# Causal attention in a decoder: the keys' turn one group later, a prologue in another order, and value products three groups back

## The chip, the cores and the metric

The kernel runs on one NeuronCore of a Trainium2 chip. The metric is the device time of one launch in microseconds, the median of several runs. Beside it stands one profiled execution, from which all rows below are read. Engines are named as in the profile: PE is TensorE (matmuls, and transposes as matmuls with the identity), PEld its weight loads, DVE is VectorE, ACT is ScalarE, POOL is GpSimd, SP is the engine that issues the DMAs.

## The reference, cut to what matters

The kernel computes two decoder layers on 8 batches of 256 tokens of width 512: linear attention, a convolution mixer, a feed-forward block, then causal attention, a cross attention and a mixture of small experts, each followed by a residual and a normalisation. The change touches the causal attention alone:

```python
qkv = jnp.einsum('bsd,de->bse', x, Wqkv)
q, k, v = jnp.split(qkv, 3, axis=-1)
q = _layernorm_scale_only(q, q_ln_scale)          # over all 512 columns
k = _layernorm_scale_only(k, k_ln_scale)
...                                               # 16 heads of 32
scores = jnp.einsum('bshd,bthd->bhst', q / jnp.sqrt(jnp.float32(HEAD_DIM)), k)
scores = jnp.where(causal, NEG_INF, scores)
attn = jax.nn.softmax(scores, axis=-1)
ctx = jnp.einsum('bhst,bthd->bshd', attn, v)
out = jnp.einsum('bsd,de->bse', ctx.reshape(B, S, D_MODEL), out_W)
```

## The kernel before

The stage is the function `l1_attention`. Each engine has its own instruction list, written out by hand, and the engines meet only through counting semaphores (`wait_ge`); nothing reorders them. A batch (b = 0 to 7) has 256 tokens, two halves of 128 (t = 0, 1), and is worked in four groups (g = 0 to 3) of four heads. `steps()` runs over all 32 groups, n = 4b + g.

While the groups of batch b are worked, batch b + 1 is made ready. A unit (`project`) is a projection of one half by a 512-column part of the weights, 12 matmuls (three passes over four blocks: high by high, high by low, low by high part). Units 0 to 3 are queries and keys of half 0, then queries and keys of half 1; units 4 and 5 are the values. They write two banks, `p_ps[0]` and `p_ps[1]`, in turn. Queries and keys are normalised: VectorE takes mean and variance and writes the centred rows (`centre`, L1494 to L1502), POOL makes the reciprocal deviation (`rstds`), ACT scales the keys with it (`keys`, L1417), TensorE turns queries and keys (`turn_q` L1661, `turn_k` L1668), and ACT and VectorE copy the turned tiles out (`turned_q` L1421, `turned_k` L1507). The queries' deviation is applied later, as the scale of the exponentials.

A group n goes through: `scores` (L1683) into the four banks of `s_ps`; `masked_scores` (L1513) on VectorE, which copies them to SBUF; `maxima` of each half; `exps` on ACT, four heads for each half (L1433); `reciprocals` on VectorE; `normalise` on POOL (L1390, half 1 of group n - 1 and half 0 of group n at step n); `turn_p` (L1697), three transposes of four heads each, of group n - 2; `copy_pt` on ACT (two) and VectorE (one); `values` (L1712) of group n - 2 at the end of step n; `round_out` on ACT (L1447) and `lo_out` on VectorE (L1542), which split the output in a high and a low part. Once a batch the output projection (`output`), the residual and the normalisation follow.

PSUM is full: `p_ps` two banks, `s_ps` four, `tr_ps` and `v_out_ps` one each. Turned tiles (x, q, k, p) borrow the banks of `s_ps` between two groups' scores (`in_spare`), so the next group's scores wait until every borrowed bank is copied out:

```python
if n:
    pe.wait_ge(masked, n)
for h in range(GH):
    if h in freed:
        pe.wait_ge(*freed.pop(h))
```

Weights come in 8 pieces through a ring of three buffers: two each for Wq, Wk, Wv and Wout. ACT rounds a piece (`round_hi`, L107) and VectorE takes what is left (`take_lo`, L112); the first three are loaded ahead, during the stage before.

Of the kernel before, what the change touches and what calls it, by code (L numbers as in the profile page):

```python
# [14 lines left out]
P = 128  # L15
B, S, D = 8, 256, 512
T = S // P
# [1233 lines left out]
def l1_attention(core, ahead, after, x, y, q_scale, k_scale):  # L1251
    nc = core.nc
    with ExitStack() as ctx:
# [39 lines left out]
        q_bank, k_bank = spare[2], spare[3]  # L1293
# [20 lines left out]
        def unit_count(b, t):  # L1314

            return t + 1 if b == 0 else 4 + t if b == 1 else 4 * b + t - 1

        def residual_count(b):

            return 4 * b + 10 if b < B - 2 else 31 + b - (B - 2)  # L1320

# [6 lines left out]
        with nc.Block() as block:  # L1328
# [30 lines left out]
            def _(pool):  # L1359
# [12 lines left out]
                def rstds(b, t):  # L1372
                    n, u = T * b + t, b % 2
                    pool.wait_ge(mv_done, 2 * n + 2)
# [32 lines left out]
            def _(act):  # L1407
# [5 lines left out]
                def keys(b, t):  # L1413
                    n = T * b + t
                    act.wait_ge(rstd_done, n + 1)
                    act.wait_ge(p_free[1], unit_count(b, t))
                    act.activation(kn[t][:], kn[t][:], ACT.Copy, scale=rstd[:, t, 1:2]).then_inc(kn_done, 1)  # L1417

                def turned_q(b, t):
                    act.wait_ge(q_turned, T * b + t + 1)  # L1420
                    act.activation(qT[b % 2][:, :, t, :], q_bank, ACT.Copy).then_inc(q_copied, 1)  # L1421
# [26 lines left out]

                for r in range(2):
                    round_x(0, r)  # L1450
                split.round_hi(act, 0, len(split.pieces))
                for t in range(T):
                    keys(0, t)
                    turned_q(0, t)
                for t in range(T):
                    values(0, t)
                for r in range(2):
                    round_x(1, r)
                for b, u, g, n in steps():
                    if n >= 3:  # L1460
                        round_out(n - 3)
                    exps(b, u, n, 0)
# [12 lines left out]
                    if g == 2 and b + 1 < B:  # L1475
                        values(b + 1, 1)
                last = NG * B - 1
# [7 lines left out]
            def _(dve):  # L1485
# [5 lines left out]
                def centre(b, t, i):  # L1491
                    n, out, row = T * b + t, (qn, kn)[i][t], (qs_row, ks_row)[i]
                    dve.wait_ge(p_mm, 6 * b + 2 * t + i + 1)
                    dve.bn_stats(st[:, t, i, :], p_ps[i][:]).then_inc(st_done, 1)  # L1494
                    if b:
                        dve.wait_ge(ve_done, n - 1)
                    dve.wait_ge(st_done, 2 * n + i + 1)
                    dve.bn_aggr(mv[:, t, i, :], st[:, t, i, :]).then_inc(mv_done, 1)
                    dve.wait_ge(mv_done, 2 * n + i + 1)
                    if b:  # L1500
                        dve.wait_ge((q_turned, k_turned)[i], n - 1)
                    dve.scalar_tensor_tensor(out[:], p_ps[i][:], mv[:, t, i, 0:1], row[:], ALU.subtract, ALU.mult)\  # L1502
                       .then_inc(p_free[i], 1)

                def turned_k(b, t):
                    dve.wait_ge(k_turned, T * b + t + 1)
                    dve.tensor_copy(kT[b % 2][:, :, t, :], k_bank).then_inc(k_copied, 1)  # L1507
# [44 lines left out]

                for r in range(2):
                    lo_x(0, r)
                split.take_lo(dve, 0, 4)
                dve.wait_ge(rows_loaded, 32)
                for i in range(2):
                    centre(0, 0, i)
                split.take_lo(dve, 4, len(split.pieces))
                for i in range(2):  # L1560
                    centre(0, 1, i)
# [3 lines left out]
                for r in range(2):  # L1565
                    lo_x(1, r)
                for b, u, g, n in steps():
# [16 lines left out]
                    if g in (1, 2) and b + 1 < B:  # L1584
                        turned_k(b + 1, g - 1)
# [6 lines left out]
                    if g == 1 and b >= 2:  # L1592
                        norm.apply(dve, b - 2)
                last = NG * B - 1
# [14 lines left out]
            def _(pe):  # L1609
# [25 lines left out]
                def project(b, unit):  # L1635
                    u = b % 2
                    i, t = (unit % 2, unit // 2) if unit < 4 else (2, unit - 4)
# [19 lines left out]
                def turn_q(b, t, n=0):  # L1657
                    in_spare(2, n, q_copied, T * b + t + 1)
                    pe.wait_ge(p_free[0], unit_count(b, t))
                    for g in range(NG):  # L1660
                        last = pe.transpose(q_bank[:, g, :], qn[t][:, g * P:(g + 1) * P], core.ident[:])  # L1661
                    last.then_inc(q_turned, 1)

                def turn_k(b, t, n=0):
                    in_spare(3, n, k_copied, T * b + t + 1)
                    pe.wait_ge(kn_done, T * b + t + 1)
                    for g in range(NG):
                        last = pe.transpose(k_bank[:, g, :], kn[t][:, g * P:(g + 1) * P], core.ident[:])  # L1668
# [50 lines left out]
                for unit in range(6):  # L1719
                    pe.wait_ge(split.lo_done, (2, 4, 4, 4, 6, 6)[unit])  # L1720
                    project(0, unit)
                for t in range(T):
                    turn_q(0, t)
                    turn_k(0, t)
                for r in range(2):
                    turn_x(1, r)
# [744 lines left out]
```

## Time and profile before

| | us |
|---|---|
| median of three runs | 2142.49 (2141.91 to 2142.78) |
| profiled execution, its own time | 2137.15 |
| its span, first to last instruction | 2135.3 |
| TensorE busy | 1864.2 (87%) |
| VectorE busy | 1249.0 (58%) |
| ScalarE busy | 920.2 (43%) |
| GpSimd busy | 288.9 (14%) |
| mean granted clock of TensorE | 0.946 of full speed |

The shares are means over six stages. The causal stage runs from 1258.9 us to about 1684 us of the span. In a timeline row the first number is the start, the second the duration, xN the number of instructions merged, and the bracket at the end gives the idle time of the engine just before and what ended it. A table by stretch gives for each engine its busy time and count, then the granted clock (1.00 is 2.4 GHz, 0.50 is 1.2 GHz), the share of the DMA engines and GB/s.

### The profile page before, as it was taken

The page shows a single profiled execution, that of the slowest core. Times are in us where ns is not written, and L with a number is a line of the kernel's source. Part 1 is how long each engine was busy: PE and PEld are TensorE (multiplying, and loading weights), DVE is VectorE, ACT ScalarE, POOL GpSimd, SP SyncE. Part 2 cuts the span into 40 slices and gives each one's busy share as a digit, 9 for nine tenths or more (in the row PEclk, how much of TensorE's full clock was granted, in tenths as well). Part 3 has the DMA queues.
Part 4 walks back from the last instruction along what each step waited for, and adds up shares of the span by engine and source line. Part 5 has one row for each costly group of instructions (what it writes and reads, how often), then busy time and mean ns, then how long its engine had stood idle before and what let it go on. Part 6 is the DMA issues. An engine that isn't in the chain of part 4 may idle for free. (4 is left out here: it accounts for less than half of the span.)

```text
span 2135.3 us, 33023 instructions
## 1 busy us (share of the span) xinstructions
PE 1864.2 (87%) x12272; PEld 1514.4 (71%) x12272; DVE 1249.0 (58%) x2330; ACT 920.2 (43%) x2376; POOL 288.9 (14%) x347
## 2 busy tenths in 40 slices
PE   6979999999966899999999967888887488889966
PEld 5869999998954788888888855666665355555543
DVE  3445444444425665654565335677776378878847
ACT  2234333333323433333332224555556388888821
POOL 0000000000001111211111001223333221111001
PEclk9989999999988899999999988899998799999988
DMA  3122000000122221111110121000001377465234
GB/s 101 51 89 70 21 21 21 21 21 21 35 60 79 84 65 40 45 35 31 40 40 16 40 80 40 11 31 31 31 20 41 112 194 173 125 159 138 80 112 138
DMA packets 86253, 136.62 MB, mean 64 GB/s; under 512 B 9480, under 2 KB 25480, under 8 KB 86096
## 3 DMA queue, kind: packets, MB, share of 16 engines
q1 hardware_dynamic: 86096, 134.52, 21.8%
q8 instruction: 99, 1.62, 0.3%
q14 instruction: 58, 0.48, 0.1%
HBM read 79.88 MB, written 21.05 MB: 47 GB/s over the span
## 5 line engine op out<-in xcount | busy, mean ns | idle before, releaser
L1941 ACT ACTIVATE e_p<-e_s_ps,e_nb 128x512 f32<-128x512 f32 x256 | 174.8, 696 | 50.7 <-DVE e_nb L1989 49.2
L1164 PE MATMUL yp<-ccy,toep 128*128 128x288 f32 x640 | 178.7, 429 | 19.7 <-POOL ccy L892 13.6
L1433 ACT ACTIVATE p<-p,nb,rq 128x128 f32<-128x128 f32 (+1 forms) x256 | 136.8, 540 | 121.0 <-DVE nb L1524 121.0
L1989 DVE TENSOR_REDUCE e_nb<-e_s_ps 128x2 f32<-128x1024 f32 x128 | 155.7, 1217 | 50.9 <-PE e_s_ps L2066 50.9
L2076 PE MATMUL e_t_ps<-ident,e_p 128*128 128x128 f32 x1024 | 145.8, 281 | 23.8 <-DVE e_pT L1996 12.8
L1164 PEld LDWEIGHTS yp<-ccy,toep 128*128 128x128 f32 x640 | 124.0, 202 | 54.5 <-POOL ccy L892 14.8
L2076 PEld LDWEIGHTS e_t_ps<-ident,e_p 128*128 128x128 f32 x1024 | 117.9, 144 | 60.3 <-issue 50.3
L80 PE MATMUL q_ps<-a_xt_hi,wq_hi 128*128 128x256 f32 x512 | 151.9, 297 | 4.1 <-DVE wo_lo L112 4.1
L1062 DVE SCALAR_TENSOR_TENSOR hm<-gu_ps,us_col,sg 128x256 f32<-128x256 f32 x88 | 42.3, 481 | 182.0 <-ACT sg L971 182.0
L82 PE MATMUL q_ps<-a_xt_hi,wq_lo 128*128 128x256 f32 x512 | 146.6, 286 | 0.0
L81 PE MATMUL q_ps<-a_xt_lo,wq_hi 128*128 128x256 f32 x512 | 146.5, 286 | 0.0
L514 ACT ACTIVATE ex<-ex 128x512 f32<-128x512 f32 x64 | 40.4, 632 | 214.1 <-DVE ex L567 214.1
L1390 POOL TENSOR_TENSOR p<-p,rs 128x512 f32<-128x512 f32 x64 | 94.1, 1470 | 246.8 <-DVE rs L1531 246.8
L231 POOL TENSOR_TENSOR n_rstd<-n_mv,eps 128x2 f32<-128x2 f32 x32 | 6.2, 195 | 894.3 <-DVE n_mv L225 894.3
L971 ACT ACTIVATE sg<-gu_ps,gs_col 128x256 f32<-128x256 f32 x88 | 41.5, 472 | 188.1 <-PE gu_ps L82 188.1
L545 DVE TENSOR_TENSOR tl<-t_ps,th 128x512 fp32r<-128x512 f32 x64 | 44.2, 691 | 132.6 <-ACT th L506 132.6
L80 PE MATMUL o_ps<-wo_hi,th 128*128 128x512 f32 x256 | 106.7, 417 | 1.9 <-DVE tl L545 1.9
L80 PE MATMUL gu_ps<-m_xt_hi,wg_hi 128*128 128x256 f32 x352 | 100.1, 285 | 8.2 <-DVE m_xt_lo L1054 8.2
L2066 PE MATMUL e_s_ps<-ks,qs 128*128 128x512 f32 x256 | 95.3, 455 | 13.1 <-DMA ks<-e_cl 11.9
L80 PEld LDWEIGHTS q_ps<-a_xt_hi,wq_hi 128*128 128x128 f32 x512 | 100.1, 195 | 4.5 <-issue 4.5
L567 DVE TENSOR_SCALAR ex<-q_ps,bq_col 128x256 f32<-128x256 f32 x128 | 55.8, 477 | 80.3 <-PE q_ps L82 80.3
L81 PE MATMUL o_ps<-wo_lo,th 128*128 128x512 f32 x256 | 101.2, 395 | 0.0
(277 smaller groups left out, 5167.5 us busy)
## 6 DMA issues: line engine op xcount, KB each, us to landing
x_after<-n_r SPq DMA_DIRECT2D x24, 512.0 KB, 3.0
toep<-padded_kernels SPq DMA_DIRECT2D x32, 256.0 KB, 3.4
qs<-e_xh SPq DMA_DIRECT2D x64, 128.0 KB, 2.6
qs<-e_xl SPq DMA_DIRECT2D x64, 128.0 KB, 2.6
ks<-e_ch SPq DMA_DIRECT2D x64, 128.0 KB, 2.6
ks<-e_cl SPq DMA_DIRECT2D x64, 128.0 KB, 2.6
x<-x_after SPq DMA_DIRECT2D x12, 512.0 KB, 4.6
x<-in_x SPq DMA_DIRECT2D x8, 512.0 KB, 4.0
```

The lines of the kernel that those rows point to most:

```text
L80: pe.matmul(out, whi, xhi, start=start, stop=False)
L81: pe.matmul(out, whi, xlo, start=False, stop=False)
L82: return pe.matmul(out, wlo, xhi, start=False, stop=stop)
L545: dve.tensor_tensor(tl[:], t_ps[:], th[:], ALU.subtract).then_inc(tl_done, 1)
L567: dve.tensor_scalar(ex[p % 2][:, h, :], q_ps[p % 2][:, h, :], bq_col[:, head:head + 1], 0.0, ALU.add, ALU.min).then_inc(mq_done, 1)
L1164: last = pe.matmul(yp[:, lo % 2, 0:NCOL], toep[h % 2][:, (lo - li) * P:(lo - li + 1) * P], ccy[h % 2][:, li, 0:NCOL], start=(li == 0), sto ...
L1390: pool.tensor_tensor(tile, tile, r, ALU.mult).then_inc(pn_done, 1)
L1433: act.activation(p[n % 3][:, h, part[t]], p[n % 3][:, h, part[t]], ACT.Exp, bias=nb[i][:, t, h:h + 1], scale=rq[u][:, t:t + 1], accum_out= ...
L1941: act.activation(pr[i][:, a, :], s_ps[i][:, a, :], ACT.Exp, bias=nb[i][:, a:a + 1], accum_out=sums[t][:, j, q:q + 1]).then_inc(e_done, 1)
L1989: dve.tensor_reduce(nb[i][:], s_ps[i][:], AX.X, ALU.max, negate=True).then_inc(nb_done, 1)
L2066: last = pe.matmul(s_ps[i][:, a, :], qs[u][:, h // HT, h % HT, q * P:(q + 1) * P], ks[u][:, h // HT, h % HT, :], start=True, stop=True)
L2076: last = pe.transpose(t_ps[a][:, k, :], pr[m % 2][:, a, k * P:(k + 1) * P], core.ident[:])
```

## The change

It has four parts, which all engines' lists follow.

1. `turn_k` and `turned_k` of batch b + 1 move from groups 1 and 2 to groups 2 and 3.
2. `values` moves from the end of a step, where it took group n - 2, to behind the scores, where it takes group n - 3. On ACT `round_out(n - 3)` moves behind `exps` of half 0.
3. The prologue (batch 0) projects queries of both halves, then keys, then values, with queries of half t in bank t and keys of half t in bank t; the turns use the bank of `s_ps` numbered t. Pieces 0 and 1 of the weights are split ahead of x, and x of batch 1 is turned between the queries' turn and the values.
4. The last two weight pieces (Wout) are split at the end of groups 1 and 2 of batch 0, on ACT and VectorE, no more in the prologue.

```diff
@@ -1290,7 +1290,8 @@
         part = (slice(0, P), slice(P, P + S))
         spare = [s_ps[:, h, :].rearrange("p (a n) -> p a n", a=NG) for h in range(GH)]
         p_bank_of = [tr_ps[:], spare[0], spare[1]]
-        q_bank, k_bank = spare[2], spare[3]
+        q_bank = lambda b, t: spare[2 if b else t]
+        k_bank = lambda b, t: spare[3 if b else t]
 
         s = lambda n: core.sem("d_" + n)
         rows_loaded, set_up, mask_zeroed, xr_loaded = s("rows_loaded"), s("set_up"), s("mask_zeroed"), s("xr_loaded")
@@ -1311,13 +1312,21 @@
                 for g in range(NG):
                     yield b, b % 2, g, NG * b + g
 
-        def unit_count(b, t):
-
-            return t + 1 if b == 0 else 4 + t if b == 1 else 4 * b + t - 1
+        def unit_count(b, i, t):
+
+            return i + 1 if b == 0 else 4 + t if b == 1 else 4 * b + t - 1
 
         def residual_count(b):
 
             return 4 * b + 10 if b < B - 2 else 31 + b - (B - 2)
+
+        def unit_bank(b, i, t):
+
+            return t if b == 0 or i == 2 else i
+
+        def unit_place(b, i, t):
+
+            return 6 * b + (T * i + t if b == 0 or i == 2 else 2 * t + i)
 
         def x_half(g):
             return {0: 0, 3: 1}[g]
@@ -1371,7 +1380,7 @@
 
                 def rstds(b, t):
                     n, u = T * b + t, b % 2
-                    pool.wait_ge(mv_done, 2 * n + 2)
+                    pool.wait_ge(mv_done, 2 * n + 2 if b else 3 + t)
                     if n >= T:
                         pool.wait_ge(kn_done, n - 1)
                     pool.tensor_tensor(rstd[:, t, :], mv[:, t, :, 1], eps1[:], ALU.add).then_inc(ve_done, 1)
@@ -1413,12 +1422,12 @@
                 def keys(b, t):
                     n = T * b + t
                     act.wait_ge(rstd_done, n + 1)
-                    act.wait_ge(p_free[1], unit_count(b, t))
+                    act.wait_ge(p_free[unit_bank(b, 1, t)], unit_count(b, 1, t))
                     act.activation(kn[t][:], kn[t][:], ACT.Copy, scale=rstd[:, t, 1:2]).then_inc(kn_done, 1)
 
                 def turned_q(b, t):
                     act.wait_ge(q_turned, T * b + t + 1)
-                    act.activation(qT[b % 2][:, :, t, :], q_bank, ACT.Copy).then_inc(q_copied, 1)
+                    act.activation(qT[b % 2][:, :, t, :], q_bank(b, t), ACT.Copy).then_inc(q_copied, 1)
 
                 def values(b, t):
                     act.wait_ge(p_mm, 6 * b + 4 + t + 1)
@@ -1446,20 +1455,22 @@
                         act.wait_ge(o_mm, T * (b - 1))
                     act.activation(oh[b % 2][:, g, :], v_ps[:], ACT.Copy).then_inc(oh_done, 1)
 
+                split.round_hi(act, 0, 2)
                 for r in range(2):
                     round_x(0, r)
-                split.round_hi(act, 0, len(split.pieces))
+                split.round_hi(act, 2, 6)
+                for t in range(T):
+                    turned_q(0, t)
+                for r in range(2):
+                    round_x(1, r)
                 for t in range(T):
                     keys(0, t)
-                    turned_q(0, t)
                 for t in range(T):
                     values(0, t)
-                for r in range(2):
-                    round_x(1, r)
                 for b, u, g, n in steps():
+                    exps(b, u, n, 0)
                     if n >= 3:
                         round_out(n - 3)
-                    exps(b, u, n, 0)
                     if g in (1, 2) and b + 1 < B:
                         keys(b + 1, g - 1)
                     if n >= 2:
@@ -1474,6 +1485,8 @@
                     exps(b, u, n, 1)
                     if g == 2 and b + 1 < B:
                         values(b + 1, 1)
+                    if n in (1, 2):
+                        split.round_hi(act, 5 + n, 6 + n)
                 last = NG * B - 1
                 round_out(last - 2)
                 for n in (last - 1, last):
@@ -1490,21 +1503,23 @@
 
                 def centre(b, t, i):
                     n, out, row = T * b + t, (qn, kn)[i][t], (qs_row, ks_row)[i]
-                    dve.wait_ge(p_mm, 6 * b + 2 * t + i + 1)
-                    dve.bn_stats(st[:, t, i, :], p_ps[i][:]).then_inc(st_done, 1)
+                    place, bank = unit_place(b, i, t), unit_bank(b, i, t)
+                    centred = 4 * b + place - 6 * b
+                    dve.wait_ge(p_mm, place + 1)
+                    dve.bn_stats(st[:, t, i, :], p_ps[bank][:]).then_inc(st_done, 1)
                     if b:
                         dve.wait_ge(ve_done, n - 1)
-                    dve.wait_ge(st_done, 2 * n + i + 1)
+                    dve.wait_ge(st_done, centred + 1)
                     dve.bn_aggr(mv[:, t, i, :], st[:, t, i, :]).then_inc(mv_done, 1)
-                    dve.wait_ge(mv_done, 2 * n + i + 1)
+                    dve.wait_ge(mv_done, centred + 1)
                     if b:
                         dve.wait_ge((q_turned, k_turned)[i], n - 1)
-                    dve.scalar_tensor_tensor(out[:], p_ps[i][:], mv[:, t, i, 0:1], row[:], ALU.subtract, ALU.mult)\
-                       .then_inc(p_free[i], 1)
+                    dve.scalar_tensor_tensor(out[:], p_ps[bank][:], mv[:, t, i, 0:1], row[:], ALU.subtract, ALU.mult)\
+                       .then_inc(p_free[bank], 1)
 
                 def turned_k(b, t):
                     dve.wait_ge(k_turned, T * b + t + 1)
-                    dve.tensor_copy(kT[b % 2][:, :, t, :], k_bank).then_inc(k_copied, 1)
+                    dve.tensor_copy(kT[b % 2][:, :, t, :], k_bank(b, t)).then_inc(k_copied, 1)
 
                 def masked_scores(n):
                     dve.wait_ge(s_mm, n + 1)
@@ -1550,20 +1565,21 @@
                 def statistics(b):
                     norm.statistics(dve, b, [(p_free[t], residual_count(b)) for t in range(T)])
 
+                split.take_lo(dve, 0, 2)
                 for r in range(2):
                     lo_x(0, r)
-                split.take_lo(dve, 0, 4)
+                split.take_lo(dve, 2, 4)
                 dve.wait_ge(rows_loaded, 32)
-                for i in range(2):
-                    centre(0, 0, i)
-                split.take_lo(dve, 4, len(split.pieces))
-                for i in range(2):
-                    centre(0, 1, i)
+                for t in range(T):
+                    centre(0, t, 0)
+                split.take_lo(dve, 4, 6)
+                for t in range(T):
+                    centre(0, t, 1)
+                for r in range(2):
+                    lo_x(1, r)
                 dve.wait_ge(set_up, 3)
                 for t in range(T):
                     turned_k(0, t)
-                for r in range(2):
-                    lo_x(1, r)
                 for b, u, g, n in steps():
                     masked_scores(n)
                     maxima(b, u, n, 0)
@@ -1581,8 +1597,8 @@
                     reciprocals(n, 0)
                     if g in (0, 3) and b + 2 < B:
                         lo_x(b + 2, x_half(g))
-                    if g in (1, 2) and b + 1 < B:
-                        turned_k(b + 1, g - 1)
+                    if g in (2, 3) and b + 1 < B:
+                        turned_k(b + 1, g - 2)
                     if g < 2 and b + 1 < B:
                         centre(b + 1, g, 1)
                     if g == 3 and b:
@@ -1591,6 +1607,8 @@
                         statistics(b - 2)
                     if g == 1 and b >= 2:
                         norm.apply(dve, b - 2)
+                    if n in (1, 2):
+                        split.take_lo(dve, 5 + n, 6 + n)
                 last = NG * B - 1
                 reciprocals(last, 1)
                 lo_out(last - 2)
@@ -1634,7 +1652,7 @@
 
                 def project(b, unit):
                     u = b % 2
-                    i, t = (unit % 2, unit // 2) if unit < 4 else (2, unit - 4)
+                    i, t = (unit // 2, unit % 2) if b == 0 else (unit % 2, unit // 2) if unit < 4 else (2, unit - 4)
                     p_bank(unit % 2)
                     if unit == 0:
                         pe.wait_ge(xl_done, 2 * b + 2)
@@ -1655,17 +1673,17 @@
                     last.then_inc(o_mm, 1)
 
                 def turn_q(b, t, n=0):
-                    in_spare(2, n, q_copied, T * b + t + 1)
-                    pe.wait_ge(p_free[0], unit_count(b, t))
+                    in_spare(2 if b else t, n, q_copied, T * b + t + 1)
+                    pe.wait_ge(p_free[unit_bank(b, 0, t)], unit_count(b, 0, t))
                     for g in range(NG):
-                        last = pe.transpose(q_bank[:, g, :], qn[t][:, g * P:(g + 1) * P], core.ident[:])
+                        last = pe.transpose(q_bank(b, t)[:, g, :], qn[t][:, g * P:(g + 1) * P], core.ident[:])
                     last.then_inc(q_turned, 1)
 
                 def turn_k(b, t, n=0):
-                    in_spare(3, n, k_copied, T * b + t + 1)
+                    in_spare(3 if b else t, n, k_copied, T * b + t + 1)
                     pe.wait_ge(kn_done, T * b + t + 1)
                     for g in range(NG):
-                        last = pe.transpose(k_bank[:, g, :], kn[t][:, g * P:(g + 1) * P], core.ident[:])
+                        last = pe.transpose(k_bank(b, t)[:, g, :], kn[t][:, g * P:(g + 1) * P], core.ident[:])
                     last.then_inc(k_turned, 1)
 
                 def scores(b, u, g, n):
@@ -1716,16 +1734,23 @@
 
                 for r in range(2):
                     turn_x(0, r)
-                for unit in range(6):
-                    pe.wait_ge(split.lo_done, (2, 4, 4, 4, 6, 6)[unit])
+                for unit in range(4):
+                    if unit % 2 == 0:
+                        pe.wait_ge(split.lo_done, unit + 2)
                     project(0, unit)
                 for t in range(T):
                     turn_q(0, t)
-                    turn_k(0, t)
                 for r in range(2):
                     turn_x(1, r)
+                pe.wait_ge(split.lo_done, 6)
+                for unit in (4, 5):
+                    project(0, unit)
+                for t in range(T):
+                    turn_k(0, t)
                 for b, u, g, n in steps():
                     scores(b, u, g, n)
+                    if n >= 3:
+                        values(n - 3)
                     if g < 3 and b + 1 < B:
                         project(b + 1, 2 * g)
                     elif g == 3 and b:
@@ -1739,14 +1764,14 @@
                         turn_x(b + 2, x_half(g), n + 1)
                     if g in (1, 2) and b + 1 < B:
                         turn_q(b + 1, g - 1, n + 1)
-                        turn_k(b + 1, g - 1, n + 1)
+                    if g in (2, 3) and b + 1 < B:
+                        turn_k(b + 1, g - 2, n + 1)
                     if g < 3 and b + 1 < B:
                         project(b + 1, 2 * g + 1)
                     elif g == 3 and b:
                         output(b - 1, 1)
-                    if n >= 2:
-                        values(n - 2)
                 last = NG * B - 1
+                values(last - 2)
                 for n in (last - 1, last):
                     for m in range(3):
                         turn_p(n, m, last + 1)
```

## Rows read from the trace of the kernel before

**Rows 1.** Busy time by stretch of the causal stage: prologue, batches 0, 1, 2-6, 3, 7.
```profile
1258.90:1300.69 41.79, 27.28 (x104) 20.97 (x105) 19.79 (x26) 14.65 (x19) 5.12 (x15) 0.73 0.38 127
1300.69:1343.28 42.59, 31.59 (x217) 23.64 (x217) 28.91 (x46) 23.04 (x73) 12.14 (x15) 0.91 0.07 24
1343.28:1391.19 47.91, 44.00 (x297) 33.53 (x297) 32.93 (x54) 28.46 (x89) 14.04 (x16) 0.86 0.01 1
1391.19:1629.93 238.74, 205.85 (x1476) 157.13 (x1472) 173.73 (x299) 134.31 (x419) 74.57 (x90) 0.93 0.09 30
1439.13:1487.07 47.94, 41.38 (x300) 31.56 (x296) 34.98 (x61) 27.02 (x85) 14.91 (x18) 0.93 0.10 34
...
1629.93:1680.40 50.47, 35.33 (x284) 25.17 (x280) 32.95 (x58) 26.03 (x85) 15.61 (x13) 0.83 0.18 63
```

**Rows 2.** Timeline, TensorE, batch 1 (first two rows) and batch 3, groups 0 and 1.
```profile
1362.99 0.78 PE L1668 MATMUL s_ps<-ident,kn 128*128 128x128 f32 x4 [1.95 <-ACT kn L1417]
...
1367.90 0.86 PE L1712 MATMUL v_out_ps<-pT,vt 128*32 128x256 f32 x16
...
1440.00 0.50 PE L80 MATMUL p_ps<-wqkv_hi,d_xt_hi 128*128 128x512 f32 x1
...
1442.90 0.60 PE L1697 MATMUL tr_ps<-ident,p 128*128 128x128 f32 x4
...
1447.70 0.86 PE L1712 MATMUL v_out_ps<-pT,vt 128*32 128x256 f32 x16
1448.49 0.94 PE L1683 MATMUL s_ps<-kT,qT 32*128 32x128 f32 x16
...
1457.97 0.63 PE L1668 MATMUL s_ps<-ident,kn 128*128 128x128 f32 x4 [3.27 <-ACT kn L1417]
...
1462.88 0.86 PE L1712 MATMUL v_out_ps<-pT,vt 128*32 128x256 f32 x16
```

**Rows 3.** Timeline, VectorE, batch 3, group 0 and parts of group 1.
```profile
1440.14 1.76 DVE L1513 TENSOR_TENSOR p<-s_ps,mask 128x1536 f32<-128x1536 f32 x1 [0.99 <-PE s_ps L1683]
...
1442.65 0.23 DVE L1524 TENSOR_SCALAR nb<-mx,nrq 128x4 f32<-128x4 f32 x1
...
1444.87 0.41 DVE L1542 TENSOR_TENSOR ol<-v_out_ps,oh 128x256 fp32r<-128x256 f32 x1
1445.20 0.68 DVE L1494 BATCH_NORM_STATS2 qk_stats<-p_ps 128x6 f32<-128x512 f32 x1
...
1446.87 0.68 DVE L1537 COPY pT<-s_ps 128x512 f32<-128x512 f32 x1
...
1451.39 1.72 DVE L1513 TENSOR_TENSOR p<-s_ps,mask 128x1536 f32<-128x1536 f32 x1
...
1464.67 1.00 DVE L239 TENSOR_SCALAR n_r<-n_r,n_mv,n_rstd 128x512 f32<-128x512 f32 x2
```

**Rows 4.** Timeline, GpSimd and ScalarE, batch 3, group 1.
```profile
1454.26 1.89 POOL L1390 TENSOR_TENSOR p<-p,rs 128x1024 f32<-128x1024 f32 x1 [1.75 <-DVE rs L1531]
...
1457.11 0.72 ACT L1417 ACTIVATE kn<-kn,qk_rstd 128x512 f32<-128x512 f32 x1 [0.95 <-POOL qk_rstd L1379]
...
1458.69 0.60 ACT L1421 ACTIVATE qT<-s_ps 128x512 f32<-128x512 f32 x1
```

**Rows 5.** Groups of instructions by shape, window of batch 3: line, tiles, count | busy, mean ns.
```profile
L1433 ACT ACTIVATE p<-p,nb,rq 128x256 f32<-128x256 f32 x17 | 10.0, 599 | 0.0
L1433 ACT ACTIVATE p<-p,nb,rq 128x128 f32<-128x128 f32 x16 | 7.7, 483 | 15.7 <-DVE nb L1524 15.7
```

**Rows 6.** Timeline of the prologue: first matmul of two projections, Wout's last piece.
```profile
1268.49 0.79 PE L80 MATMUL p_ps<-wqkv_hi,d_xt_hi 128*128 128x512 f32 x1 [4.03 <-DVE wqkv_lo L112]
...
1283.59 1.06 ACT L107 ACTIVATE wout_hi<-ring 128x1024 fp32r<-128x1024 f32 x1 [5.32 <-DMA ring<-in_wout]
...
1284.68 1.22 DVE L112 TENSOR_TENSOR wout_lo<-ring,wout_hi 128x1024 fp32r<-128x1024 f32 x1 [2.43 <-ACT wout_hi L107]
...
1287.66 0.76 PE L80 MATMUL p_ps<-wqkv_hi,d_xt_hi 128*128 128x512 f32 x1 [4.96 <-DVE qn L1502]
```

## The prediction, on record before the changed kernel ran

> **What bounds the kernel now.** I read the engine shares first, then the table by stretch, then the order of instructions inside one batch. TensorE leads (1864.2 us busy of 2135.3, VectorE 1249.0), but the change touches only the causal stage, about 421 us [rows 1], so only that stage's waits count. Batches 2 to 6 take 238.74 us together and batch 3 alone 47.94, in which TensorE works 41.38 and VectorE 34.98 [rows 1]: neither is full, so a chain sets the pace.
>
> The chain is at the keys' turn. In group 1 TensorE has finished the queries' turn and stands 3.27 us at the keys' turn for ACT's scaled keys (L1417), and the next projection then runs at the lower clock: from the keys' turn to the value products 4.91 us [rows 2]. At full clock a projection takes 2.90 and a turn about 0.4 (projection, three turns of p, one of x and a second projection: 2.90 + 4.80, less 1.3 for p) [rows 2], so 3.35 would do and 1.56 is the clock's price. Group 2 repeats it; groups 0 and 3 have none and take about 9.3 (group 0: 1439.13 to 1448.49 [rows 1, 2]). Hence 47.94 = four groups of work, 37.9, and twice about 5.
>
> Why are the keys late? ACT scales them after POOL's rstd, and POOL's rstd stands behind POOL's normalisation of the previous group, which starts only when VectorE's masked scores of this group and its first maxima are through: masked scores start 1451.39, normalisation 1454.26, keys 1457.11 to 1457.83 [rows 3, 4].
>
> **The change, part by part.** Times below count from the start of a group's scores; m is the start of its masked scores.
>
> *Keys a group later.* In group 2 the keys of half 0 were scaled one group earlier, in group 3 those of half 1, so neither turn waits. TensorE's own demand becomes scores 0.87, values 0.79, projection 2.90, p 1.31, x or q 0.36, projection 2.97 = 9.2; groups 2 and 3 hold one turn more, 9.63. Sum 37.6: 10.3 of the 47.94 goes off TensorE. What is late next?
>
> But the scores of the next group still wait for ACT's queries (L1421) and pT copies, because they sit in the score banks, and these copies stand on ACT behind the same keys instruction. So the chain stays and only moves its end. Walk of a steady batch:
>
> Group 0: scores end 0.94, m = 1.01. VectorE's list there is 11.25 long (1440.14 to 1451.39 [rows 3]) and nothing leaves it. New is that ACT rounds the output behind the exponentials of the first half instead of ahead. Exponentials start at m + 2.78 (0.23 after 1442.65 [rows 3]) and take 4 x 0.483 = 1.93 [rows 5], the rounding ends at about m + 5.1, and the residue (L1542), so far at m + 4.73 [rows 3], waits 0.4. VectorE is through at 1.01 + 11.25 + 0.40 = 12.66; this is m of group 1 wherever TensorE stands (it starts group 1 at 9.6, behind the copy of x's low half).
>
> Group 1: from m to the end of the queries' copy was 1459.29 - 1451.39 = 7.90 [rows 3, 4], with semaphore time 8.04 to 8.09; no entry of that chain is removed. The scores of group 2 start at 12.66 + 8.09 = 20.75. TensorE could have started them at 9.6 + 9.2 = 18.8, so an idle of 1.9 remains. VectorE's list in group 1: 5.07 to the first centring, 1.67 twice (1445.20 to 1446.87), pT copy and a reciprocal 0.7, normalised rows 1.00 less 0.08 overlap (TensorE's wait no longer splits the list): 10.0, plus 0.4 for the residue [rows 3]. It ends at 23.06.
>
> Group 2: m = 23.06, the same chain plus ACT's first value copy (0.49): 8.58, so group 3 starts at 31.64. Group 3 has 8.1 of VectorE work and no rstd, so TensorE sets it: 9.63. Period 41.27.
>
> *The clock.* An idle of 1.95 before a keys' turn in batch 1 also gave 4.91 to the value products [rows 2], so I charge 1.56 to TensorE behind the remaining 1.9. Group 2 then needs 9.63 + 1.56 = 11.19 against the chain's 10.89: 0.3 more, period 41.56. Ends: 41.27 with no low clock; 43.1 if the clock is low in group 3 too. Batches 2 to 6: 4 x 41.56 + 40.5 (the last has no x to turn, as before) = 206.7 against 238.74: **-32.0**.
>
> The Trainium skill has a rule against this change, in TensorE: Matmul & The Clock Gate, section "A second HAM failure mode: psum-queue depth-cycling": short idles between groups of matmuls are enough to swing the clock between its levels, without one long wait. By it every batch would have two low stretches, the 43.1 above; with the 1.95 row alone the sum is 41.56. Idles of 0.10 before value products [rows 2] don't show it.
>
> *Values of the group three steps back.* They move from behind the second projection to behind the scores. In batches 0 to 6 it is the same 0.79 of work elsewhere (nothing, since scores already wait for the same pT copies; cover gone, 0.8 a group). In batch 7 there is no projection, and the loop is scores, masked scores, exponentials, pT, values, scores. Values leave it: three times 0.8; one product comes on top of the last group, 0.8 to 1.5. I take **-1.3** (ends -2.4 and 0), on 50.47.
>
> *Prologue.* It is 41.79 long at clock 0.73 [rows 1]. Wq is split while x is still landing, so the first projection starts when x's low half is ready, about 1265.95, not 1268.49 [rows 6]: 2.5. The values' projection stood 4.96 for VectorE's centring behind four weight splits, and started at the low clock [rows 6], 1.9 more: both go, since the two units take other banks and the k weights and queries come first; the wait for ACT's last weight piece (5.32 idle until 1283.59 [rows 6]) leaves the path. Turned again: projections q, q end about 1274.7, k, k 1280.4 (k waits for centring of q, done by then), q and x turns 1282.7, v, v 1288.4, k turns 1289.2, copies 1290.1. First scores at 1290.2 instead of 1300.69 (start of batch 0 [rows 1]): **-10.5**. Ends: -5 if the sixth weight piece, needed at 1282, lands as late as the eighth did; -11.5.
>
> *Batches 0 and 1*, 42.59 and 47.91 [rows 1]. The two Wout pieces now sit at the end of groups 1 and 2 of batch 0: the residue of each waits for ACT's rounding (1.06 [rows 6]) behind the second exponentials (4 x 0.599 = 2.4 [rows 5]) and costs 1.22 itself [rows 6]. Group 0: m 1.0, centring done and m of group 1 at 9.2. Group 1: VectorE's own list is 8.2, with the piece 11.6, m = 20.8. Group 2: own chain 8.6 + 1.0, with the piece 13.7, m = 34.5. Group 3: 8.05 (pT, x and keys' copies), end 42.5: as long as before (42.59 [rows 1]), so what the keys' turn frees, the pieces take: 3.4 + 4.1. Ends: 0 to 7.5 if they hide. Batch 1 starts on a low clock, VectorE's centring waits for slow projections (+2.5), no statistics or rows yet (-2.5): 41.3. Together 83.8 against 90.50: **-6.7**.
>
> **Sum.** -32.0 - 1.3 - 10.5 - 6.7 = -50.5. The profiled execution took 2137.15 (span 2135.3), 5.34 below the median of the three runs; it becomes 2086.6, and the median 2142.49 - 50.5 = **2092.0**.
>
> **Rivals.**
> - *The idles that remain drop the clock twice a batch.* For it: 1.95 sufficed once; the new batch has about 1.9 and, if the first drop fails, 1.3. Against: after a drop in group 2 TensorE is the later one and has no idle. 43.1 x 5, batch 1 +1.6: 9.3 more, 2101. Chance 0.15.
> - *TensorE becomes the bound.* The period is its 37.6 if queries' copies come early. Against: POOL's normalisation and rstd stay ahead of them. 206.7 - 5 x 3.9, batch 1 -3: 2069. Chance 0.06.
> - *The pieces and the prologue give other values*: Wout hidden, 2084.5 (0.06); prologue held by a weight's DMA, 2097.5 (0.06).
> - *Slower.* ACT's rounding behind the exponentials holds VectorE's residue and pT copy, and so the next scores, in all 32 groups. At the walk's 0.4 it is in the sum; the gains are used up when it holds 0.4 + 50.5 / 32 = 2.0 us in each. That needs value products ending after m + 6.3, where they end before m + 1 at full clock. Chance 0.02, at 2145 or more.
> - *It does not do what it says* (keys' turn still waits): the keys of half 0 are ready 1.6 before group 2 starts and used 6 after. Under 0.01.
>
> **How the numbers follow.** The forecast has 0.64; 2092 is its value, its own range 2086 to 2098. For 8 in 10 I go to both neighbours, the ends of prologue and pieces added: 2076 to 2106. Differences under 0.2% (4.3 us) a measurement of this kernel can't tell from none. Faster by more: all but the slower rival, 0.96; within 0.01; slower 0.03.
>
> **What would show it.** First scores about 10 us earlier; no idle before L1668's successor; scores L1683 of group 2 idle near 1.9 for ACT's qT; VectorE's L1542 0.4 after L1524's end; batches 41 to 42 apart with the long groups 1 and 2 at 11 each; first group of batch 1 still at the low clock. I am wrong if the periods near 38 or 44, or if the masked scores of batch 0, group 3 start much before 34 us after its first scores.

## The result and the profile after

The changed kernel takes 2090.97 us (median of four runs, 2084.84 to 2093.04), the kernel before in the same sessions 2142.2: ratio 0.976, 95% interval 0.9735 to 0.9786. The profiled execution has a span of 2083.0 us against 2135.3.

The table by stretch of the changed kernel answers to [rows 1]: the whole causal stage from x's first turn, prologue, batches 0, 1, 2 to 6, 3 and 7.

```profile
1263.68:1626.10 362.42, 316.20 (x2368) 242.08 (x2368) 288.67 (x481) 222.22 (x679) 119.33 (x142) 0.96 0.13 44
1263.68:1289.52 25.84, 23.01 (x105) 18.80 (x105) 16.51 (x24) 11.08 (x15) 2.45 (x8) 0.87 0.63 198
1289.52:1331.29 41.77, 29.23 (x200) 22.58 (x201) 30.87 (x48) 24.99 (x76) 12.15 (x15) 0.96 0.04 13
1331.29:1371.56 40.27, 39.29 (x296) 29.95 (x297) 32.26 (x53) 27.58 (x87) 14.11 (x16) 0.96 0.01 2
1371.56:1577.41 205.85, 191.12 (x1473) 147.23 (x1473) 175.00 (x298) 132.62 (x420) 74.98 (x90) 0.98 0.10 34
1413.04:1454.54 41.50, 39.29 (x298) 29.95 (x297) 35.30 (x60) 26.70 (x85) 15.00 (x18) 0.96 0.11 40
...
1577.41:1626.10 48.69, 33.56 (x297) 23.51 (x296) 34.02 (x58) 25.95 (x85) 15.63 (x13) 0.89 0.19 66
```

The same stretch of the kernel before, from x's first turn to the last output projection:

```profile
1262.50:1680.73 418.23, 344.38 (x2368) 260.46 (x2368) 288.32 (x481) 226.48 (x681) 120.36 (x142) 0.89 0.11 38
```

So the stage gives 418.23 - 362.42 = 55.8 us; the stages around it give 3.5 back in this execution (the stage starts 1.2 later, and what follows it takes 2.3 more) without any change of theirs. TensorE's busy time falls too, 344.38 to 316.20, with the same 2368 matmuls: the clock is 0.96 where it was 0.89.

TensorE in batch 3, starts of the four groups' scores (L1701, which was L1683) and the keys' turn (L1686, was L1668), answers to [rows 2]:

```profile
1413.04 0.94 PE L1701 MATMUL s_ps<-kT,qT 32*128 32x128 f32 x16
...
1422.65 0.94 PE L1701 MATMUL s_ps<-kT,qT 32*128 32x128 f32 x16 [0.37 <-DVE d_xt_lo L1502]
...
1433.73 1.32 PE L1701 MATMUL s_ps<-kT,qT 32*128 32x128 f32 x16 [1.84 <-ACT qT L1430]
1434.98 1.51 PE L1730 MATMUL v_out_ps<-pT,vt 128*32 128x256 f32 x16
...
1441.58 0.60 PE L1686 MATMUL s_ps<-ident,kn 128*128 128x128 f32 x4
...
1444.91 0.94 PE L1701 MATMUL s_ps<-kT,qT 32*128 32x128 f32 x16
...
1451.21 0.60 PE L1686 MATMUL s_ps<-ident,kn 128*128 128x128 f32 x4
```

Neither keys' turn waits. What is left in batch 3 is one idle of 1.84 before group 2's scores, ended by ACT's copy of the queries, and behind it a short low clock (value products 1.51, not 0.86). Batch 2 is the same; batches 4 to 6 have no low clock there and a second idle of 1.28 before group 3's scores. VectorE, ACT and POOL around it answer to [rows 3, 4]:

```profile
1419.14 0.42 DVE L1557 TENSOR_TENSOR ol<-v_out_ps,oh 128x256 fp32r<-128x256 f32 x1 [0.28 <-ACT oh L1456]
...
1425.68 1.72 DVE L1528 TENSOR_TENSOR p<-s_ps,mask 128x1536 f32<-128x1536 f32 x1
```

```profile
1428.55 1.90 POOL L1399 TENSOR_TENSOR p<-p,rs 128x1024 f32<-128x1024 f32 x1 [1.74 <-DVE rs L1546]
```

```profile
1431.41 0.72 ACT L1426 ACTIVATE kn<-kn,qk_rstd 128x512 f32<-128x512 f32 x1 [0.69 <-POOL qk_rstd L1388]
...
1432.99 0.60 ACT L1430 ACTIVATE qT<-s_ps 128x512 f32<-128x512 f32 x1
```

It is the chain of the kernel before, from masked scores (1425.68) over POOL's normalisation to the keys and the queries' copy (1433.59), 7.91 us against 7.90 [rows 3, 4]; only its last link now releases the scores. And VectorE's residue has a wait that it had not: 0.28 for ACT's rounding.

### The profile page after: what moved, and what is told of

Read it like the earlier page. It is cut to its first block and busy times, and to the rows that moved or that the text cites. A ratio compares the mean times of both kernels' runs of the same rounds, so it can differ in the third digit from the quotient of the medians.

```text
span 2083.0 us, 33021 instructions
## 1 busy us (share of the span) xinstructions
PE 1838.2 (88%) x12272; PEld 1497.9 (72%) x12272; DVE 1252.9 (60%) x2330; ACT 919.0 (44%) x2376; POOL 287.7 (14%) x347
## 5 line engine op out<-in xcount | busy, mean ns | idle before, releaser
L1966 ACT ACTIVATE e_p<-e_s_ps,e_nb 128x512 f32<-128x512 f32 x256 | 175.3, 699 | 52.5 <-DVE e_nb L2014 51.2
L567 DVE TENSOR_SCALAR ex<-q_ps,bq_col 128x256 f32<-128x256 f32 x128 | 55.8, 477 | 80.2 <-PE q_ps L82 80.2
```

The source lines that it names most:

```text
L567: dve.tensor_scalar(ex[p % 2][:, h, :], q_ps[p % 2][:, h, :], bq_col[:, head:head + 1], 0.0, ALU.add, ALU.min).then_inc(mq_done, 1)
L1966: act.activation(pr[i][:, a, :], s_ps[i][:, a, :], ACT.Exp, bias=nb[i][:, a:a + 1], accum_out=sums[t][:, j, q:q + 1]).then_inc(e_done, 1)
```

## The experiments

For each: the causal stage from x's first turn on, and batch 3, from the table by stretch of its profile. The changed kernel has 362.42 and 41.50, the kernel before 418.23 and 47.94. Whole times spread by several us between executions of one kernel, so I read parts from the stage.

**The keys' turn alone**, on the kernel before:

```diff
-                    if g in (1, 2) and b + 1 < B:
-                        turned_k(b + 1, g - 1)
+                    if g in (2, 3) and b + 1 < B:
+                        turned_k(b + 1, g - 2)
...
-                        turn_k(b + 1, g - 1, n + 1)
+                    if g in (2, 3) and b + 1 < B:
+                        turn_k(b + 1, g - 2, n + 1)
```

> Only part 1 (keys' turn and copy a group later) on the kernel before. Theory of the walk (a chain from VectorE through POOL and ACT to the next scores stays): batches 2 to 5 come 40.8 to 41.5 apart, as in the changed kernel, and the time is about 2142 - 34 - 6 = 2102, prologue as before (38.2 us from x's first turn to the first scores). Rival (the value products behind the scores carry part of the gain): batches 43 or more apart, over 2112.

```profile
1262.87:1629.93 367.06, 322.66 (x2368) 246.72 (x2368) 286.90 (x481) 225.44 (x681) 120.39 (x142) 0.94 0.13 44
1300.99:1336.91 35.92, 29.78 (x217) 22.70 (x217) 28.59 (x46) 23.66 (x75) 12.13 (x15) 0.94 0.08 28
1418.12:1458.63 40.51, 38.10 (x300) 29.48 (x296) 34.78 (x61) 26.86 (x84) 14.92 (x18) 1.00 0.11 41
```

2090.52 us, ratio 0.9757 (0.972 to 0.9794). These few lines give 51.2 of the stage's 55.8 us, and in the whole time they can't be told from the full change (0.976, 0.9735 to 0.9786). A batch is 40.51, below the range that I gave and below the changed kernel, at full clock throughout, and batch 0 (second row) takes 35.92 where both other kernels have some 42. The rival, that value products carry part of it, falls. I had expected the whole time 11 us longer, with 34 and 6 us gained; the stage gained 37.2 in batches 2 to 6, 6.7 in batch 0 and 7.2 in batch 1.

Against this run, the three other parts make the prologue 12.3 shorter, batch 0 5.9 longer (Wout's pieces), batch 1 0.4 shorter, batches 2 to 6 4.3 longer and batch 7 2.1 shorter: 4.6 in all.

**The keys' turn back in groups 1 and 2**, the rest of the change kept (the same lines undone in the changed kernel):

> The changed kernel with part 1 alone undone. If the keys' turn is what the steady batches gained by: batches 47.5 to 48.5 apart again and about 2129. If prologue and value products did it: under 2110.

```profile
1267.79:1668.29 400.50, 335.25 (x2368) 254.90 (x2368) 289.97 (x481) 222.75 (x679) 119.05 (x142) 0.91 0.12 40
1432.22:1479.75 47.53, 41.13 (x298) 31.55 (x297) 35.39 (x60) 26.82 (x87) 14.96 (x18) 0.93 0.10 35
...
1451.45 0.63 PE L1686 MATMUL s_ps<-ident,kn 128*128 128x128 f32 x4 [3.17 <-ACT kn L1426]
```

(The last row is from the timeline of TensorE.) 2129.34 us, ratio 0.994 (0.9919 to 0.996). The wait of 3.17 us for the keys and the period of 47.5 are back, as expected. From both sides the keys' turn is worth 38 to 51 us of the stage; the other three parts together are worth 17.7 without it and 4.6 on top of it.

**Value products and rounding back** (part 2 undone in the changed kernel: `values(n - 2)` at the end of a step, `round_out` ahead of `exps`):

```diff
                     scores(b, u, g, n)
-                    if n >= 3:
-                        values(n - 3)
...
+                    if n >= 2:
+                        values(n - 2)
                 last = NG * B - 1
-                values(last - 2)
```

> The changed kernel with part 2 undone: value products of the group two back at the end of a step, rounding ahead of the exponentials. Theory: scores waited for the same copies anyway, and the rounding's hold of 0.4 in two groups goes, so batches 2 to 5 are 0.2 to 0.8 SHORTER than 41.5 and only batch 7 gets about 1 to 2 longer: within 3 us of the changed kernel. Rival: values ahead of the scores lengthen every group by 0.8, batches 43 or more apart, 2100 or more.

```profile
1265.25:1623.21 357.96, 315.87 (x2368) 242.89 (x2368) 285.52 (x481) 222.93 (x680) 118.81 (x142) 0.96 0.13 45
1411.36:1451.88 40.52, 38.10 (x300) 29.48 (x296) 34.79 (x61) 26.86 (x84) 14.93 (x18) 1.00 0.11 41
1572.41:1623.21 50.80, 35.65 (x284) 25.18 (x280) 32.97 (x58) 25.80 (x83) 15.60 (x13) 0.83 0.18 63
```

2088.09 us (2083.49 to 2092.17). Steady batches are 1.0 shorter (I gave 0.2 to 0.8) and batch 7 is 50.80 against 48.69, 2.1 longer. Part 2 makes the stage 4.5 us longer. Batches 2 to 6 take 201.56 and batch 7 50.80, as with the keys' turn alone (201.53 and 50.79): neither the prologue nor the pieces touch them.

**Wout's pieces in the prologue's wait**, on the changed kernel:

```diff
                 for t in range(T):
                     keys(0, t)
+                split.round_hi(act, 6, 8)
...
-                    if n in (1, 2):
-                        split.round_hi(act, 5 + n, 6 + n)
...
                     lo_x(1, r)
+                split.take_lo(dve, 6, 8)
                 dve.wait_ge(set_up, 3)
...
-                    if n in (1, 2):
-                        split.take_lo(dve, 5 + n, 6 + n)
```

> The changed kernel with Wout's two pieces split in the prologue, in VectorE's 4.5 us wait for the keys' turn, not at the ends of groups 1 and 2 of batch 0. Theory (the pieces cost 3.4 and 4.1 in batch 0): first scores at the same place, masked scores of group 3 about 7 earlier, batch 1 starts 7 to 8 earlier, time 7 to 8 us shorter. Rival (they hide behind TensorE, or the prologue pays them): under 2 us.

```profile
1268.29:1623.98 355.69, 316.00 (x2368) 241.48 (x2368) 288.67 (x481) 222.16 (x679) 119.08 (x142) 0.96 0.13 45
1294.18:1329.02 34.84, 27.52 (x201) 21.05 (x201) 28.50 (x46) 23.11 (x74) 12.14 (x15) 1.00 0.05 16
...
1623.98:2087.70 463.72, 365.92 (x2656) 234.45 (x2656) 334.72 (x593) 292.63 (x728) 66.59 (x61) 0.90 0.51 137
```

2088.77 us (2078.35 to 2089.49). Batch 0 falls from 41.77 to 34.84 at the same prologue (25.9): the pieces did cost 6.9 us. The median moves by 2.2 only (I gave 7 to 8), or by 4.9 if each is taken against the kernel before in its own series (2142.2 and 2144.93): in the profiled execution the stages behind, untouched, took 463.72 us (third row), where the changed kernel's took 456.90 (its row stands below). Where the pieces cost it, the timeline of VectorE in the changed kernel shows; each waits for ACT's rounding, 2.05 and 6.12 us:

```profile
1308.84 1.23 DVE L112 TENSOR_TENSOR wout_lo<-ring,wout_hi 128x1024 fp32r<-128x1024 f32 x1 [2.05 <-ACT wout_hi L107]
...
1322.18 1.23 DVE L112 TENSOR_TENSOR wout_lo<-ring,wout_hi 128x1024 fp32r<-128x1024 f32 x1 [6.12 <-ACT wout_hi L107]
```

**The rounding alone back ahead of the exponentials** (value products stay behind the scores), on ACT:

```diff
-                    exps(b, u, n, 0)
                     if n >= 3:
                         round_out(n - 3)
+                    exps(b, u, n, 0)
```

> The changed kernel, but the rounding of the output (ACT) back ahead of the exponentials; the value products stay behind the scores. Theory (the rounding is what holds VectorE's residue 0.28 to 0.4 in every group): no idle before L1557's residue, batches 2 to 5 at 40.4 to 41.1 instead of 41.5, and batch 7's first groups 0.2 to 0.3 shorter each. Rival (the place of the value products costs, not the rounding): batches stay at 41.3 to 41.5.

```profile
1261.86:1619.82 357.96, 317.26 (x2368) 242.34 (x2368) 286.38 (x481) 223.83 (x679) 118.81 (x142) 0.95 0.13 45
1411.73:1452.53 40.80, 37.98 (x297) 29.30 (x296) 34.88 (x60) 26.94 (x84) 14.93 (x18) 1.00 0.12 40
...
1432.33 0.94 PE L1701 MATMUL s_ps<-kT,qT 32*128 32x128 f32 x16 [1.93 <-ACT qT L1430]
```

2082.53 us, one run. 0.7 of the 1.0 that part 2 costs a batch is the rounding's place, 0.28 the value products'. Batch 7's first three groups went from 7.27, 7.99, 7.72 to 6.89, 7.55, 7.61.

The 0.28 can be read from VectorE in group 0, by the second centring, of the keys; the first row is from the kernel with both orders back, the second from this one:

```profile
1420.37 0.69 DVE L1509 BATCH_NORM_STATS2 qk_stats<-p_ps 128x6 f32<-128x512 f32 x1
...
1421.01 0.70 DVE L1509 BATCH_NORM_STATS2 qk_stats<-p_ps 128x6 f32<-128x512 f32 x1 [0.19 <-PE p_ps L82]
```

From the batch's start that is 9.01 and 9.28. Value products behind the scores put both projections 0.79 later, and VectorE, which did not wait here before, now waits for the second one. The 0.27 stays to the end of the batch: group 1's masked scores start at 12.27 and 12.55, the last group's at 31.90 and 32.17. The stage is 357.96 in both kernels all the same: here batch 7 is 45.75 against 50.80, in part by a last group at clock 1.00 and not 0.91, and prologue and batch 1 are 3.5 longer.

**POOL's rstd ahead of its normalisation; VectorE's pT copy ahead of the centring; both with the rounding first.** Three kernels:

```diff
+                    if g in (1, 2) and b + 1 < B:
+                        rstds(b + 1, g - 1)
                     if n:
                         normalise(n - 1, 1)
-                    if g in (1, 2) and b + 1 < B:
-                        rstds(b + 1, g - 1)
...
+                    if n >= 2:
+                        copy_pt(n - 2)
                     if g < 2 and b + 1 < B:
                         centre(b + 1, g, 0)
                     if g == 3 and b:
                         residual(b - 1, 0)
-                    if n >= 2:
-                        copy_pt(n - 2)
```

> The changed kernel with POOL's rstd ahead of its normalisation of the group before. If the chain over POOL were the only one: group 1 shortens by 0.7 or more, batches 40.5 or less. My walk: VectorE's pT copy behind the centring is ready only 0.1 before the queries' copy, so group 1 shortens by 0.1 to 0.2 and batches by 0 to 0.4.

> The changed kernel with VectorE's pT copy ahead of the centring and the residual. My walk: the POOL and ACT chain still sets the next scores, batches within 0.2 of 41.5. If VectorE's order alone were the limit: 40.5 or less.

> The edits of the last three together. If two parallel chains end within 0.1 us of each other, only together do they shorten group 1: walk 9.4 + 9.9 + 10.5 + 9.6 = 39.4 (39.0 to 40.0). If their effects only add up, batches are no shorter than 41.5 less the sum of the three alone.

Batch 3 and the scores of its group 2, for the first, the second and the three edits together:

```profile
1414.33:1455.80 41.47, 39.30 (x298) 30.05 (x297) 35.25 (x60) 26.48 (x85) 15.27 (x18) 0.96 0.11 40
...
1435.01 1.08 PE L1701 MATMUL s_ps<-kT,qT 32*128 32x128 f32 x16 [1.81 <-DVE pT L1552]
```

```profile
1416.08:1457.57 41.49, 39.29 (x298) 30.24 (x297) 35.29 (x60) 26.69 (x85) 14.97 (x18) 0.96 0.11 40
...
1436.77 0.94 PE L1701 MATMUL s_ps<-kT,qT 32*128 32x128 f32 x16 [1.84 <-ACT qT L1430]
```

```profile
1404.55:1444.28 39.73, 37.96 (x297) 29.31 (x297) 34.89 (x60) 26.71 (x84) 15.28 (x18) 1.00 0.12 41
...
1424.09 0.94 PE L1701 MATMUL s_ps<-kT,qT 32*128 32x128 f32 x16 [0.88 <-ACT qT L1430]
```

One run each, 2089.5, 2091.72 and 2068.88 us. Alone the two edits give 0.03 and 0.01 us in batch 3. With rstd first, the same idle of 1.8 is ended by VectorE's pT copy; otherwise by ACT's queries: two parallel chains that end together, in group 1. That group takes 11.08 in the changed kernel, 11.06 and 11.08 with one edit, 11.36 with the rounding first, and 10.30 with all three. No run has the two edits without the rounding, so that this pair is what shortens the group is read from the change of the releaser and not tried. All three give 1.77 in batch 3, where the sum of the three alone is 0.74. The walk had 39.4.

Part of that difference is the clock. Group 2 of batch 3 ran with a low stretch in the changed kernel and with either edit, and without one in the other two. In batch 5, where none of the five has one, the gains are 0.48 (rounding), 0.83 (rstd), 0.01 (pT copy) and 1.57 (all), so the sum of the three alone is 1.32. And rstd first does show alone: in group 2 of batch 5 (changed kernel, then rstd first), and in batch 0 (third row), which took 41.77 in the changed kernel:

```profile
1516.50:1527.47 10.97, 9.68 (x76) 7.56 (x77) 8.55 (x15) 7.40 (x23) 5.05 (x7) 1.00 0.27 98
...
1517.99:1528.12 10.13, 9.69 (x76) 7.55 (x77) 8.53 (x15) 6.45 (x21) 5.33 (x7) 1.00 0.32 106
1293.42:1333.07 39.65, 29.14 (x201) 22.47 (x201) 30.86 (x48) 24.77 (x76) 12.23 (x15) 0.96 0.04 14
```

**All of it**, with the keys ahead of the exponentials on ACT too (their rstd is ready by then):

```diff
+                    if g in (1, 2) and b + 1 < B:
+                        keys(b + 1, g - 1)
                     exps(b, u, n, 0)
-                    if g in (1, 2) and b + 1 < B:
-                        keys(b + 1, g - 1)
```

> The three edits of the run before together, Wout's pieces in the prologue's wait, and ACT's keys ahead of the exponentials. Theory: the queries' copy comes 0.6 earlier in groups 1 and 2, so batches 2 to 5 at 38.5 to 39.1; batch 0 at about 34; the causal stage 336 to 343 us, and the time about 2065 (2060 to 2072). Rival (TensorE or VectorE already bound at 39.7): batches stay at 39.7 and only Wout's 7 us come off.

```profile
1264.30:1604.66 340.36, 315.48 (x2368) 240.53 (x2368) 286.14 (x481) 223.74 (x679) 121.03 (x142) 0.97 0.14 47
1290.97:1323.86 32.89, 27.60 (x201) 21.01 (x201) 28.41 (x46) 23.11 (x74) 12.26 (x15) 1.00 0.05 16
1402.21:1441.41 39.20, 38.17 (x298) 29.29 (x297) 34.90 (x60) 26.87 (x84) 15.30 (x18) 1.00 0.12 42
```

2070.33 us (2067.64 to 2073.39), ratio to the kernel before 0.965 (0.9629 to 0.967): it beats both. The single run before it, with the three edits, was no slower (2068.88), though its stage is 9.8 us longer (350.19): the stages behind took 457.42 us there and 463.84 here. The stage lies in the range given, the batch at 39.20 just above it, with TensorE busy 38.17 of 39.20. Of the rival only this much is left: the step from 39.73 is 0.5, not 0.9.

## Why the prediction was right

2092.0 was predicted and 2090.97 measured. The mechanisms are mostly those of the prediction; that the median comes within 1.0 us is luck. The stage gave 5.3 us more than the terms add up to, the stages around it took 3.5 back in the profiled execution, and that execution lies 6.1 us below its median, where that of the kernel before lay 5.3 below the median of three. By its terms, all in the causal stage:

| term | predicted | measured in the profile |
|---|---|---|
| batches 2 to 6 | -32.0 | 238.74 - 205.85 = -32.9 |
| batch 7 | -1.3 | 50.80 - 48.69 = -2.1 |
| prologue | -10.5 | x's first turn to first scores 38.19 to 25.84: -12.3 |
| batches 0 and 1 | -6.7 | 90.50 - 82.04 = -8.5 |
| sum | -50.5 | -55.8 in the stage, -52.3 in the span |

*The keys' turn and what is late next.* Right in kind, shown by undoing it and by doing it alone. The walk put group 1's masked scores at 12.66 after the batch's start, the scores of group 2 at 20.75 and those of group 3 at 31.6 to 31.9; in batch 3 they are at 12.64, 20.69 and 31.87. The idle of 1.9 that it left is 1.84.

*The rounding's hold.* Right: 0.28 of idle, or 5.10 from the masked scores' start where it was 4.73, the 0.4 of the walk. It was priced within the period, but I did not say what it means for part 2: as a whole this part loses 1.0 a batch and wins 2.1 once. The cost of "nothing" for the value products was wrong in its reason too: I looked only at what they do to the scores' wait, and they delay the projections, for which VectorE then waits (0.19 of idle, 0.28 a batch).

*Batch 7.* Its first three groups are 2.9 shorter together (the walk: three times 0.8) and its last 0.8 longer, as said. The 2.1 is no firm size: in the kernel with rstd first, an edit that leaves batch 7's order as it is, batch 7 takes 46.63 against 48.69, with the last group at clock 1.00 and not 0.91.

*The clock.* The term was 0.3 a batch. In batch 3 group 2 took 11.18 with the clock low for a moment, in batch 4 10.96 without: 0.2. The rival with two drops a batch is refuted; none of batches 2 to 6 had more than one. The prediction let the Trainium skill (TensorE: Matmul & The Clock Gate, "A second HAM failure mode: psum-queue depth-cycling") speak for it, but that section tells of a kernel whose short idles came often enough to swing the clock, and does not say how often that is; two low stretches a batch were my reading of it. Idles this rare do not bear the reading out: batch 3's clock is 0.96 in the changed kernel and 1.00 with the rounding first, in spite of idles of 1.93 and 0.89.

*Prologue.* The mechanisms hold: the first projection starts 3.5 us after x's turn (predicted the same), and nothing but the keys' copy is waited for afterwards. The size was 1.8 too small: the walk gives the first two projections 8.75 (to 1274.7), and they took 7.26, 4.47 for the first, in which the low clock ended, and 2.95 for the second; the turns of queries and x took 1.5 and not 2.3. The DMA end of the bounds did not come; all six pieces are rounded at 1274.1, the values' projection starts at 1281.5. No run undoes the new order alone; that it, and not the pieces' leaving, gives the 12.3 is shown by the run with the pieces back in the prologue, which is as short (25.89).

*Batches 0 and 1.* 42.5 and 41.3 were predicted, 41.77 and 40.27 measured. Batch 1 does start at the low clock: its first group takes 10.74 at 0.84, where it took 12.08 at 0.74.

*Wout's pieces.* I charged 7.5; taking them out of the loop gives 6.9 to 6.5 (41.77 to 34.84; 39.38 to 32.89 with the three edits, which has the keys' edit in it too). So the rival "Wout hidden" falls, and against the prologue's wait as their place part 4 is a loss of that size, which part 3's gain covers.

*TensorE as the bound* falls for the changed kernel, at 41.5 against 37.6, and holds nearly in the last experiment, where it is busy for 38.17 of 39.20.

*Slower* and *does not do what it says* are refuted by the rows above.

What stays open is why the clock fell behind the idle of batch 3 and not behind nearly the same idle of batch 4.

## What to carry to other kernels

When an engine waits in the middle of its list for a result that goes through other engines, move its use a step on, and then walk the same chain again to whatever it releases next: here 6.4 us a batch stayed (7.4 with this part alone) of the 10.3 that left TensorE's list, and the rest showed up as idle at the scores. If two chains end at the same wait, test them together; at that wait each alone may show nothing. A change that bundles four edits may hold two that pay and two that cost: read each from its own stage, not from the whole time, and compare stretches at the same granted clock.

## What the runs showed of the hardware

The granted clock does not follow from the length of an idle alone. Scores behind an idle of 1.84 us took 1.32 in batch 3 of the changed kernel, and behind 1.82 in batch 4 0.94:

```profile
1475.23 0.94 PE L1701 MATMUL s_ps<-kT,qT 32*128 32x128 f32 x16 [1.82 <-ACT qT L1430]
```

With the rounding first, 1.93 of idle left them at 0.94 in batch 3, whereas 1.95 in the kernel before was followed by 4.91 us to the value products [rows 2]. Among batches 2 to 6, group 2 has a low stretch (clock 0.85) behind this idle of 1.82 to 1.94 in two in the changed kernel, in three with Wout's pieces moved and in four with the pT copy first, and in none with the rounding first, at 1.93 to 1.95.

A small VectorE instruction stretches beside POOL's normalisation. The scaling of the second maxima, 128x4, takes 0.23 us in group 0 of batch 0, where POOL is idle (first row), and 0.85 to 0.86 in all 31 other groups of the changed kernel:

```profile
1294.42 0.23 DVE L1539 TENSOR_SCALAR nb<-mx,nrq 128x4 f32<-128x4 f32 x1
...
1429.61 0.86 DVE L1539 TENSOR_SCALAR nb<-mx,nrq 128x4 f32<-128x4 f32 x1
```

In each of the 31 it ends 0.01 to 0.03 after the normalisation (here 1430.47, and 1428.55 + 1.90 = 1430.45), while the reduction just ahead of it, under the same normalisation, takes 1.19 as against 1.21 without. That is 0.6 us a group in VectorE's list, the same before and after; its cause was not tried.

Code that no edit touches differs by more than some parts of the change. The stages behind the causal one, in the changed kernel:

```profile
1626.10:2083.00 456.90, 358.72 (x2656) 229.16 (x2656) 335.45 (x593) 291.90 (x728) 66.59 (x61) 0.92 0.52 139
```

They took 456.90 us at clock 0.92 here and 463.72 at 0.90 with Wout's pieces moved, 6.8 more; and that kernel's stage began 4.6 later. So its profiled execution is the longer one by 4.7 in spite of a stage that is 6.7 shorter. Over the eleven profiled executions these stages took 454.57 to 463.84, at 0.92 to 0.90. What set the clock there was not tried.
